# A graph network's later convolutions: the first destination tile waits for the source parts group by group

## The reference

```
hw  = h @ W
out = segment_sum(norm[edge] * hw[src[edge]], dst[edge]) + b      # norm = dinv[src] * dinv[dst], self loops included
```

## Time and profile before

| | |
|---|---|
| median of 3 runs | 6212.26 us |
| lowest, highest | 6204.62, 6234.20 us |
| profiled execution, its own time | 6224.82 us |
| its span, first to last instruction | 6223.0 us |
| mean granted TensorE clock | 0.889 of full |
| PE busy | 4880.2 us (78%) |
| DVE busy | 3745.3 us (60%) |

### The profile page before, as it was taken

How to read it: one execution, slowest core, us unless ns; L and a number is a source line. 1 busy time by engine, 2 the same in 40 slices (tenths; PEclk the granted TensorE clock), 3 DMA queues, 4 the chain that set the end, 5 groups by cost and what they waited for, 6 DMA issues and landing times.

```text
span 6223.0 us, 95155 instructions
## 1 busy us (share of the span) xinstructions
PE 4880.2 (78%) x32966; PEld 2860.3 (46%) x32966; DVE 3745.3 (60%) x6197; ACT 2462.4 (40%) x4261; POOL 2861.2 (46%) x3038
## 2 busy tenths in 40 slices
PE   4888899979999656565555565565559999999999
PEld 3777777767777433233333333233433333333334
DVE  7999523242244445444444444454379999999998
ACT  5777300010000223232322233232127777777777
POOL 3000000000000366666666666666317777777777
PEclk9999999989999777777777777777679999999999
DMA  2333586857878333343343433333101111111111
GB/s 62 145 155 155 186 268 211 267 153 244 263 215 267 94 118 117 115 120 118 112 120 116 121 114 117 119 116 109 26 24 53 52 56 50 56 53 54 56 50 33
DMA packets 296193, 759.01 MB, mean 122 GB/s; under 512 B 81000, under 2 KB 183464, under 8 KB 289704
## 3 DMA queue, kind: packets, MB, share of 16 engines
q1 hardware_dynamic: 217352, 595.36, 29.7%
q0 software_dynamic: 78624, 160.79, 9.8%
HBM read 589.77 MB, written 166.22 MB: 121 GB/s over the span
## 4 chain that ended last, share of the span: by engine, by line
PE 54%; another core or an unknown queue 15%; DVE 11%; issue 9%; POOL 7%; ACT 3%; DVEq 2%; DMA 0%; ACTq 0%; SPq 0%; POOLq 0%
PE p_e L1012 19%; PE p_e L1137 12%; PE p_tr L1150 9%; POOL GA L716 6%; PE p_mm L1121 3%; PE p_e L1044 2%; PE p_e L1050 2%; PE p_mm L977 1%; DVE VA L1621 1%; ACT GA L1343 1%; DVE GA L1621 1%; PE p_tr L1044 1%; DVE R L1621 1%; DVE GA L1623 1%
## 5 line engine op out<-in xcount | busy, mean ns | idle before, releaser
L716 POOL DMA_INDIRECT GA<-table_mg,VA x1568 | 1484.6, 947 | 2210.0 <-DMA table_mg<-VA 1424.1
L2000 DVE TENSOR_TENSOR VA<-VA,p_mm 128x1024 f32<-128x1024 f32 (+1 forms) x1274 | 1418.7, 1156 | 135.3 <-POOL VA L815 121.9
L815 POOL TENSOR_SCALAR VA<-VA 128x1024 f32<-128x1024 f32 (+1 forms) x1274 | 1241.6, 993 | 473.4 <-ACT VA L1394 468.9
L1044 PE MATMUL p_e<-BD,EA 128*128 128x384 f32 x896 | 398.4, 597 | 534.2 <-ACT GA L1343 502.9
L1394 ACT ACTIVATE VA<-p_e 128x1024 f32<-128x1024 f32 (+1 forms) x637 | 621.2, 975 | 354.3 <-PE p_e L1137 354.2
L1847 DVE SCALAR_TENSOR_TENSOR R<-R,kp,M 128x97 f32<-128x97 f32 x1568 | 513.4, 327 | 360.5 <-issue 269.3
L1150 PE MATMUL p_tr<-VA,GA 128*32 128x512 f32 (+1 forms) x5096 | 648.3, 581 | 0.4 <-DVE VA L2000 0.2
L1012 PE MATMUL p_e<-GA,VA 128*128 128x288 bf16 x4802 | 609.5, 287 | 11.2 <-DVEq L1769 11.2
L1012 PE MATMUL p_e<-GA 128*128 128x288 bf16 x4802 | 608.5, 287 | 10.8 <-DVEq L1769 10.8
L1820 DVE TENSOR_TENSOR M<-GA,p_mm 128x1344 f32<-128x1344 f32 x112 | 174.1, 1554 | 732.5 <-ACT GA L1343 716.0
L1050 PE MATMUL p_e<-GA,C 128*128 128x384 f32 x896 | 428.3, 636 | 217.7 <-DMA GA<-table_mg,VA 217.7
(11 more groups left out here) (221 smaller groups left out, 7276.9 us busy)
## 6 DMA issues: line engine op xcount, KB each, us to landing
GA<-adj SPq DMA_DIRECT2D x98, 800.0 KB, 4.7
VA<-adj SPq DMA_DIRECT2D x98, 800.0 KB, 4.7
run_m<-R SPq DMA_DIRECT2D x112, 700.0 KB
GA<-adj SPq DMA_DIRECT2D x98, 768.0 KB, 4.5
VA<-adj SPq DMA_DIRECT2D x98, 768.0 KB, 4.5
H<-adj SPq DMA_DIRECT2D x56, 896.0 KB, 5.1
adj<-GA SPq DMA_DIRECT2D x25, 1568.0 KB, 5.2
adj<-VA SPq DMA_DIRECT2D x24, 1568.0 KB, 5.2
```

The costliest lines, as they stand in the source:

```text
L716: pool.indirect_dma_start(out=to, out_offset=None, in_=of, in_offset=bass.IndirectOffsetOnAxis(ap=at, axis=0)).then_inc(s, 16)
L815: pool.tensor_scalar(e, e, HIGH, LOW, ALU.min, ALU.max).then_inc(clipped, 1)
L1044: mm = pe.matmul(p_h[k][0:CH, 0:4 * D], EA[:, h, k // 2, :], BD[:, 2 * (k % 2):2 * (k % 2) + 2, :, :].rearrange("p a b f -> p (a b f)"), s ...
L2000: dve.tensor_tensor(e, e, p_mm[n % 2][:, 0:across(b)].unsqueeze(1).to_broadcast([P, 2, across(b)]), ALU.mult).then_inc(weighed, 1)
```

## The change

PE no longer waits at the head of `adjacency(n)` for all parts. In its first destination tile, ahead of source tiles 0, 4, 8, ..., 48, it waits until that group's parts are made. The semaphore `parts_ready` is counted up by the last instruction of each `split_group`, in place of once for each convolution, so 13 times in each. Convolution 0's wait becomes one for 13.

```diff
@@ PE, count_pairs (convolution 0)
-                pe.wait_ge(parts_ready, 1)
+                pe.wait_ge(parts_ready, GROUPS)
                 pe.wait_ge(lists_kept, 2 * SETS)
@@ PE, adjacency(n) (convolutions 1 to 4)
-                pe.wait_ge(parts_ready, n + 1)
                 m = n - 1
...
                         pe.wait_ge(block_landed[b][c], landed)
                         for s in range(lo, hi):
+                            if first(d) and s % GRP == 0:
+                                pe.wait_ge(parts_ready, n * GROUPS + s // GRP + 1)
                             mm = pe.matmul(p_e[b][:, 0:PARTS * D], blk[b][:, s * P:(s + 1) * P],
@@ DVE, mark_pairs
                 dve.sem_inc(conv_used, 1)
-                dve.sem_inc(parts_ready, 1)
@@ DVE, split_group
-                dve.tensor_tensor(parts[:, group, 2, :], rest, parts[:, group, 1, :], ALU.subtract)
+                dve.tensor_tensor(parts[:, group, 2, :], rest, parts[:, group, 1, :], ALU.subtract).then_inc(parts_ready, 1)
```

## The result

| | before | after |
|---|---|---|
| median | 6234.20 us (17 runs) | 6186.17 us (17 runs) |
| lowest, highest | 6204.62, 6247.28 | 6180.08, 6216.30 |
| ratio, 95% interval | | 0.9931 [0.9919, 0.9944] |
| span of the profiled execution | 6223.0 us | 6183.5 us |
| start of convolution 1 to end of convolution 4 | 1325.6 us | 1307.2 us |

The time measured, 6186.2 us, lies on the forecast 6185.5 and inside the range. That agreement is better than the reasoning behind it. The forecast took 26.8 us off a median of three runs, 6212.3 us, and the 17 runs of before have their median 22 us higher. The whole gain is 0.69%, some 43 us, by the ratio; the two medians lie 48.0 us apart (the ratio is not their quotient). The case "faster by over 0.5%", which had 26%, came true. About 24 us of the gain are where the forecast put them. The rest, some 20 us, had no rival that named it.

What follows compares the result with a forecast made beforehand. PE bounds the kernel through the convolutions' matmuls, idling ahead of convolutions 1 to 4. Idle time 21.9 us plus clock 4.9 us make 26.8 us, so 6212.3 us becomes 6185.5 us; range 6173 to 6203.5 us.

Steps and rivals of the forecast that it cites:

- faster by over 0.5%: Whole kernel: case that the time falls below 6181.2 us, a gain over about 31.1 us; chance 26%.
- The idle time: Head of convolutions 1 to 4: PE's four waits for DVE's parts go, 21.9 us gained.
- The clock term: First tiles of convolutions 1 to 4: 4.9 us of 9.0 us lost to half clock come back.
- I count back the excess of convolutions 2 and 3 [...] and none of 1 and 4: First tiles: 2.45 + 2.47 us return where the clock fell in the idle time, none where it fell before.
- a fall at another place than after 699 and 1726: Sign that the clock term is wrong: the clock falls elsewhere than after these times (us), ahead of convolutions 1 and 4.
- The rule of the page "TensorE: Matmul & The Clock Gate": First tiles: rival that the idle gap causes every clock fall, so all 9.0 us return; gain 30.9 us, chance 20%.
- The sum: Whole kernel: 21.9 us idle time plus 4.9 us clock, 26.8 us off 6212.3 us, giving 6185.5 us.
- What adds nothing: Convolutions: PE's added waits in first tiles and DVE's increments on L1729 cost nothing; at 0.01 us per increment, 0.7 us.
- Removed are five separate increments on DVE; nothing is late for them: DVE in the convolutions: dropping the old separate counts of parts_ready changes nothing; no gain or cost counted.
- After convolution 4 everything is moved earlier as a whole: Stages behind convolution 4: they only shift earlier, with no gain or loss of their own.
- The baseline: Whole kernel: the gain is taken off 6212.3 us, the median of the runs shown, not the profiled execution's 6224.8 us.

Runs made afterwards that it cites:

- e12_after: The changed kernel once more, no edit, against the kernel before: ratio 0.9926, 6194.7 us beside 6241.8 us.
- e7_after_padded: The changed kernel plus five spare DVE increments where the kernel before had its separate ones: ratio 0.9964 to the kernel before, 5915.3 us beside 5939.5 us.
- e4_filler: The kernel before plus ten matmuls of constants ahead of PE's wait at the head of adjacency(n): ratio 0.9998 to the kernel before, 6217.1 us.
- e3: The changed kernel with a wait for all 13 groups put back at the head of adjacency(n): ratio 0.9976 to the kernel before, 6201.1 us.
- e5: The changed kernel with one wait for all groups at the head of adjacency(n) replacing tile 0's thirteen: ratio 0.9977 to the kernel before, 5917.1 us.
- e10: The changed kernel plus five spare DVE increments in one place right ahead of attention: ratio 0.9960 to the kernel before, 5915.0 us.
- the interleaved kernel: The changed kernel with PE doing tile 0's matmuls between dense-stage products, and tile 1's partly early: ratio 0.9915 to the kernel before, 5880.1 us.
- e9_before_last: The kernel before plus two matmuls of constants in each of the first eight steps of attention's last block: ratio 0.9970 to it, 5920.0 us.

## Why the prediction was right, and where it was not

**The idle time: right.** All four waits are gone, none came in their place, and no wait inside tile 0 holds. The stretches between convolutions 1 and 2 and between 3 and 4 are 5.5 and 6.1 us shorter. Between 2 and 3 it is only 3.7 us, because the dense stage there ran at half clock for longer (44.4 against 34.1 us); e12_after, the same program, has 73.1 us for that stretch, 5.7 less than before.

**The clock term: right in kind, too large in size.** Forecast was that 4.9 of the 9.0 us of slow start come back, at convolutions 2 and 3. Taken from matmul to matmul, before and after, the first tiles took 7.63 + 8.57 + 8.59 + 8.70 = 33.5 us and take 8.35 + 8.26 + 6.00 + 7.68 = 30.3 us, so 3.2 came back of the 9.5 that lie over four tiles of 6.00. (The forecast took them from weight load to weight load, and tile 1's first weights are loaded ahead of its first matmul, so its 9.0 is some 0.4 short.) The step that failed is "I count back the excess of convolutions 2 and 3 [...] and none of 1 and 4". Convolution 1 lost 0.7 us, 2 gave back 0.3, 3 gave back 2.6, and 4 gave back 1.0. By the forecast's own sign, a fall at another place than after 699 and 1726, the term was wrong about convolutions 2 and 4: at 2 the clock fell in the dense stage this time, at 4 it fell only after tile 0 had begun, and at 3 it stayed up. Which junction keeps its clock changes from execution to execution; e12_after's four convolutions took 296.8, 296.5, 295.7 and 296.1 us and e7_after_padded's 294.0, 295.7, 295.7 and 294.2, first to last matmul. e4_filler shows that the fall needs no long idle gap. The rule of the page "TensorE: Matmul & The Clock Gate" of the Trainium skill (section "HAM oscillation — how this bites in real kernels"), by which it is the long idle gap that costs the clock, would have given all of it; about a third came.

**The sum: 26.8 forecast, some 24 measured.** In the traces 24.9 - 1.0 = 23.9 us: 20.7 of idle time (5.4 ahead of convolution 1, then 5.5, 3.7 and 6.1) and 3.2 of clock. By e7_after_padded, in which the junctions are all that is changed, 24.2 us in the medians and 21 by the ratio.

**What adds nothing: right at the place, wrong for the program.** The thirteen waits and the increments on L1729 cost nothing. "Removed are five separate increments on DVE; nothing is late for them" is the step that failed. Nothing is late for them in the convolutions, but without them the clock holds in attention's last block, four milliseconds later, in nearly all runs, and with them it falls in most, as far as the runs' times tell. That is about 20 us, and 0.23 to 0.40% by the ratios (e3, e5, and the changed kernel against e7 and e10). "After convolution 4 everything is moved earlier as a whole" was wrong with it.

**The baseline.** The forecast took the median of three runs at its word. The lowest of them may have been free of the fall, as the profiled execution was (last stage 1587.1 us); this is not shown. With the 17 runs' median of 6234.2, the sum would have given 6207, outside the range at its upper end. A baseline that was 22 us too low and a gain of some 20 us that nobody had counted cancelled, and that is luck.

What stays open: how five instructions of DVE decide whether the clock falls at one place in attention. They did it from both places that were tried, the instructions just ahead of the fall are the same with and without it, and the profiled execution of the kernel before and that of e4_filler had the increments and not the fall. So they shift a likelihood and not a wait.

## What to carry to other kernels

Where an engine waits once for all of a producer's pieces and could work on the first of them, count the idle time in the waits, then ask at which clock it will start: here the first was worth some 21 us and the second 3. An engine that works with small gaps can lose its clock before the long gap comes, so fill the small gaps too, with real work: the interleaved kernel got another 14 us that way. And where a ratio is larger than the changed stage can give, compare two kernels that differ only in instructions without effect, and read every run's time and mean clock together, before a cause is made up for the stage. The mean clock alone misleads: here a stretch at half clock early in the execution lowered it and cost next to nothing.

## What the runs showed of the hardware that was not expected

- In attention's last block the clock of one and the same program either stays at full or falls to half for some 80 us, to the end: 1587 against 1610 us for the last stage. A gap of 0.75 us of PE stands just ahead of that place in both cases.
- Five increments of a semaphore that nobody waits for, on DVE, make that fall the usual case: 24 of 5940 us.
- Sixteen matmuls of constants in the first eight steps of that block keep the clock at full and gain 20 us net in a kernel of 5940 us (e9_before_last).
